# Causal mask added to the diagonal score blocks of four heads in one VectorE operation, row maxima taken two heads at a time from the masked scores

## What is computed

```
scale = D ** (-0.5)
scores = jnp.einsum('bqhd,bkhd->bhqk', sq, sk) * scale
causal = jnp.tril(jnp.ones((n, n), dtype=bool))
scores = jnp.where(causal[None, None], scores, jnp.finfo(scores.dtype).min)
attn = jax.nn.softmax(scores, axis=-1)
y = jnp.einsum('bhqk,bkhd->bqhd', attn, sv)
o = 0.5 * y + 0.5 * o_gla
```

## Time and profile before

| | |
|---|---|
| median of 3 runs | 945.17 us (944.21 to 946.2) |
| the profiled execution | 944.21 us, of which the trace spans 941.6 us |
| PE busy | 901.8 us (96%) |
| PEld busy | 712.3 us (76%) |
| DVE busy | 678.3 us (72%) |
| ACT busy | 661.8 us (70%) |
| POOL busy | 635.0 us (67%) |

### The profile page before, as it was taken

How to read it: one execution, slowest core, us unless ns; L and a number is a source line. 1 busy time by engine, 2 the same in 40 slices (tenths; PEclk the granted TensorE clock), 3 DMA queues, 4 the chain that set the end, 5 groups by cost and what they waited for, 6 DMA issues and landing times. The chain is left out here.

```text
span 941.6 us, 18334 instructions
## 1 busy us (share of the span) xinstructions
PE 901.8 (96%) x5145; PEld 712.3 (76%) x5145; DVE 678.3 (72%) x2016; ACT 661.8 (70%) x2146; POOL 635.0 (67%) x603
## 2 busy tenths in 40 slices
PE   7899999999999999999999999999999998888997
PEld 4677778787777777777777777787777766677886
DVE  4877867676767676768686969786888857574447
ACT  6687777777777777777776868687776766333655
POOL 6967676767666667677786767877676988443441
PEclk9999999999999999999999999999999999997999
DMA  7101100000000000710000001001003111133347
GB/s 263 35 12 29 29 24 1 6 13 8 1 0 0 0 0 7 210 28 1 1 2 1 1 1 43 1 2 32 1 17 105 62 39 57 57 109 95 109 126 232
DMA packets 30969, 41.46 MB, mean 44 GB/s; under 512 B 3230, under 2 KB 25631, under 8 KB 30624
## 3 DMA queue, kind: packets, MB, share of 16 engines
q1 hardware_dynamic: 27472, 31.98, 11.5%
q0 software_dynamic: 3408, 8.43, 2.5%
HBM read 24.72 MB, written 16.59 MB: 44 GB/s over the span
## 5 line engine op out<-in xcount | busy, mean ns | idle before, releaser
L1662 POOL TENSOR_TENSOR qd<-eqk,eg 128x512 f32<-128x512 f32 x63 | 75.0, 1190 | 133.2 <-issue 128.6
L631 PE MATMUL OA<-wT,V 128*128 128x512 f32 x320 | 149.2, 597 | 0.0
L847 ACT ACTIVATE S<-S,nm 128x128 f32<-128x128 f32 (+3 forms) x256 | 126.4, 494 | 8.2 <-DVE nm L1082 7.4
L1082 DVE CUSTOM_DVE_ANT_0 S<-S,maskb 128x128 f32<-128x128 f32 (+3 forms) x256 | 118.2, 518 | 15.2 <-PE S L585 12.3
L885 ACT ACTIVATE eqk<-qkv,nmx 128x128 f32<-128x128 f32 x320 | 124.3, 396 | 4.5 <-DVE nmx L1157 4.4
L1650 POOL TENSOR_TENSOR eqk<-eqk,rse 128x640 f32<-128x640 f32 x63 | 79.5, 1262 | 60.2 <-DVE rse L1200 37.0
L631 PEld LDWEIGHTS OA<-wT,V 128*128 128x128 f32 x320 | 59.7, 191 | 68.9 <-issue 68.9
L1116 DVE TENSOR_TENSOR pr<-S,rl 128x256 f32<-128x256 f32 (+3 forms) x128 | 105.5, 825 | 4.5
L1639 POOL TENSOR_TENSOR rp<-qkv,cos 128x640 f32<-128x640 f32 x64 | 99.5, 1555 | 7.7 <-ACT qkv L875 7.7
L1642 POOL TENSOR_TENSOR rp<-rp,rt 128x640 f32<-128x640 f32 x64 | 99.4, 1553 | 5.0
L1639 POOL TENSOR_TENSOR rt<-qkv,sin 128x640 f32<-128x640 f32 x64 | 99.3, 1552 | 0.0
(11 more groups left out here) (265 smaller groups left out, 2451.7 us busy)
## 6 DMA issues: line engine op xcount, KB each, us to landing
qkv<-slot_x SPq DMA_DIRECT2D x39, 129.0 KB
slot_x<-zero SPq DMA_DIRECT2D x3, 1290.0 KB, 15.3
stage<-in_wgu SPq DMA_DIRECT2D x8, 352.0 KB, 3.1
stage<-in_wqkv SPq DMA_DIRECT2D x6, 384.0 KB, 3.9
xraw<-in_x_cols SPq DMA_DIRECT2D x16, 128.0 KB, 2.5
acc<-in_x_rows SPq DMA_DIRECT2D x1, 2048.0 KB, 10.8
dn_w<-in_wdn SPq DMA_DIRECT2D x1, 2048.0 KB, 8.1
pr<-plane SPq DMA_DIRECT2D x8, 256.0 KB
```

Source lines behind the costliest of these rows:

```text
L631: last = pe.matmul(OA[:, :], V[:, j, :], wT[:, j, :], start=(c == 0 and j == 0), stop=(j == c))
L847: nc.scalar.activation(S[:, h, 0:n], S[:, h, 0:n], ACT.Exp, bias=nm[:, h:h + 1], scale=-1.0, accum_out=ls[:, h:h + 1]).then_inc(s_exp, 1)
L1082: nc.vector.tensor_tensor_reduce(out=S[:, h, 0:n], in0=S[:, h, 0:n], in1=maskb[:, N - n:N], scale=-1.0, scalar=FAR, op0=ALU.add, op1=ALU.m ...
L1662: nc.gpsimd.tensor_tensor(qd[:, par, 0:512].rearrange("p (h d) -> p h d", d=128), eqk[:, par, 0:512].rearrange("p (h d) -> p h d", d=128), ...
```

## The change

The four calls of `score_max` in a unit become one call of `mask_scores` and two of `score_max`. `mask_scores` adds the triangular block to the diagonal blocks of all four heads in one tensor operation (128 x 4 x 128 elements, in place in PSUM) and waits for the scores of all four heads. `score_max` is a plain row maximum over the n columns of two heads, with the sign turned, that waits for the mask. The custom operation with its accumulator read-out is gone, and ACT's exp no longer negates its input. In units c = 0, `o_low` of the group before, which stood between heads 1 and 2, now stands ahead of the mask.

```
-                    act.wait_ge(s_nm, 4 * u + 1 + h)
-                    nc.scalar.activation(S[:, h, 0:n], S[:, h, 0:n], ACT.Exp, bias=nm[:, h:h + 1], scale=-1.0,
+                    act.wait_ge(s_nm, 4 * u + 1 + h)
+                    nc.scalar.activation(S[:, h, 0:n], S[:, h, 0:n], ACT.Exp, bias=nm[:, h:h + 1],
                                          accum_out=ls[:, h:h + 1]).then_inc(s_exp, 1)
...
-            def score_max(g, c, h):
+            def mask_scores(g, c):
+
+                u = C * g + c
+                d = slice(P128 * c, P128 * (c + 1))
+                dve.wait_ge(s_sc, 4 * u + 4)
+                later(dve, s_exp, 4 * u)
+                nc.vector.tensor_tensor(S[:, :, d], S[:, :, d], maskb[:, N - P128:N].rearrange("p (o t) -> p o t", o=1)
+                                        .to_broadcast([P128, GQ, P128]), ALU.add).then_inc(s_mk, 1)
+
+            def score_max(g, c, pair):
 
                 u = C * g + c
                 n = P128 * (c + 1)
-                dve.wait_ge(s_sc, 4 * u + 1 + h)
-                later(dve, s_exp, 4 * u)
-                nc.vector.tensor_tensor_reduce(out=S[:, h, 0:n], in0=S[:, h, 0:n], in1=maskb[:, N - n:N], scale=-1.0,
-                                               scalar=FAR, op0=ALU.add, op1=ALU.min, accum_out=nm[:, h:h + 1]).then_inc(s_nm, 1)
+                h = slice(2 * pair, 2 * pair + 2)
+                dve.wait_ge(s_mk, u + 1)
+                nc.vector.tensor_reduce(nm[:, h], S[:, h, 0:n], AX_X, ALU.max, negate=True).then_inc(s_nm, 2)
...
                 if c:
                     update_state(g, c)
+                if c == 0 and not first:
+                    o_low(g - 1, C - 1)
+                mask_scores(g, c)
                 score_max(g, c, 0)
                 score_max(g, c, 1)
-                if c == 0 and not first:
-                    o_low(g - 1, C - 1)
-                score_max(g, c, 2)
-                score_max(g, c, 3)
```

More of the change, by code:

```diff
@@ L267, in layer_kernel @@
         s_sc, s_nm, s_exp, s_rl, s_pn = (sem(n) for n in ("s_sc", "s_nm", "s_exp", "s_rl", "s_pn"))
+        s_mk = sem("s_mk")
         s_at, s_am, s_pt, s_wta, s_wtd = (sem(n) for n in ("s_at", "s_am", "s_pt", "s_wta", "s_wtd"))
```

## The result

| | before | after |
|---|---|---|
| median | 945.68 us (944.21 to 947.31) | 1004.77 us (1002.7 to 1005.7) |
| span of the profiled execution | 941.6 us | 1002.3 us |
| mean granted TensorE clock | 0.988 | 0.976 |
| PE busy / DVE busy | 901.8 / 678.3 us | 922.2 / 717.9 us |

The ratio is 1.062, with a 95% interval of 1.061 to 1.064. The kernel is 59 us slower; 38 were forecast, and the time lies above the range. I cut both traces into the 64 units, at the first score matmul of each. The start of unit 63 moved by 60.5 us. The table gives what the units became longer, and what the prediction had for them (units 0 to 58, and the tail apart).

What follows compares the result with a forecast made beforehand. PE was taken as the bound. New waits 26.3 (c = 3) + 7.3 (c = 2) + 1.6 (c = 0) + 1.1 (c = 1) + 1.6 (tail) = 38 us gave 983 us; 8 in 10 is 971 to 1000.

Steps and rivals of the forecast that it cites:

- PE sets the pace, and each new wait adds its length: Mid-attention PE is busy 99.69 of 100 us, so every wait it lacks today adds its length to the time.
- Unit c = 3, 1.9 us: Mask waits for head 3, so `gc` comes late and PE waits 1.9 us ahead of L604; fourteen units, 26.6 us.
- the clock falls after the new stops: Rival, chance 0.26: TensorE's clock drops behind c = 3 stops, 1.5 us each; 994 us if half, 1004 if all.
- Unit c = 1, "nothing", hidden by 0.4 us: First exp waits for ACT's other work, hiding mask and maximum by 0.4 us; only two router-late units pay, 0.55 each.
- What is queued behind: Later work on DVE, ACT and POOL: `qd` stays ready, 0.1 to 0.2 us early in c = 0; DVE gets 0.4 us more per unit.
- Unit c = 0, 0.06 us: `gc` ends just after L604's present start: 0.06 us in fifteen units, 0.7 in unit 0, 1.6 in all.
- Any tenth more on DVE or ACT in c = 0 shows: Cover in c = 0 is gone after the change, so any further tenth there shows in the time.
- Unit c = 2, 0.65 us: Second `pr` ends later, so L613 waits 0.65 us in eight units and 0.3 on average in seven: 7.3 us.
- The tail, 1.6 us: From group 14's last unit POOL and a DMA also hold PE: of 4.9 us new waits, 1.6 remain.
- Smaller waits: Rival, chance 0.10: mask and maxima at lower bounds, c = 3 costs 1.6 and c = 2 0.4; 974, down to 965 us.
- a gain: Rival, chance 0.04: the wait is covered and PE's present waits on DVE go, or fewer operations save time; 940 to 945 us.
- no change: Rival, chance 0.04: exps are late for other reasons in all units, as in c = 1; 945 us.

Runs made afterwards that it cites:

- the filler: Changed kernel, in c = 3 the gated matrix moved behind the projection and five matmuls of zeros put into PE's stop: 996.07 us, ratio 1.053.
- the run with c = 1 alone: Kernel before with the new form (one mask, maxima of two heads) in units c = 1 only: 948.27 us, ratio 1.003.
- The control run: Changed kernel with the gated matrix of units c = 3 moved behind the projection, without added matmuls of zeros: 1003.86 us, ratio 1.063.
- the run with `gc` first: Changed kernel with the clamp of the gate sums ahead of both normalisations in every unit: 985.45 us, ratio 1.042.

## Why the prediction was wrong in size

*PE sets the pace, and each new wait adds its length.* Right. PE went from 99.69 to 94.36 busy us in 100, in stops released by `gc` and `pr`.

*Unit c = 3, 1.9 us.* The mechanism and the place were right, and the size nearly: 1.9 in the first two units, 2.1 in the others, 2.7 us more in 14 units. Three small terms were short. From the end of the mask to the maximum, two instructions of one engine with a semaphore between them, it is 0.10 us (322.63 to 322.73), where I put 0.03; from `gc` to L605 0.06; and the twelve matmuls of L605 take 1.52 us behind a stop, where they took 1.42.

*The rival "the clock falls after the new stops".* **This is the step that failed**, as I weighed it: "Against it: 1.78 is the nearer row." The sum of 983 us puts the clock at nothing, and it cost 11.5 us in c = 3; without these the time would lie inside the range. My stops came out at 1.84, and behind 7 of 15 the clock fell; 0.26 was too small a chance, and its 1.5 us a unit is 1.6 to 1.7. In the changed kernel and the two other runs with stops of 1.84 to 1.87 us in c = 3, 23 of 45 brought the clock down. In the five runs whose stops in c = 3 were at most 1.27 us, none of the 75 did. That it is the stop is shown by the filler: same waits, same arrival of `gc`, no fall.

The row of 1.78 us was read rightly, but it did not hold for c = 3. Its stop, in unit 2, is 1.51 to 1.82 us long in all fourteen traces, and the clock fell behind none of them. Nor does the length of a stop decide alone elsewhere. Behind the stop for `qd` in unit 60, 1.98 to 2.29 us in six traces, the clock fell in four; in unit 57 it fell in the runs with first stops of 1.50 and 1.58 us, each with a second of 0.79, and in two of the three with 1.84 and 0.80. Among equal stops, their place in time goes with what happens. In each trace all low stretches begin whole multiples of one interval apart. Of the 26 stops of 1.84 to 1.87 us in c = 3 that begin in about one half of that interval, 23 brought the clock down, and of the 19 in the other half none. I chose the halves after looking, and no run moves a stop on purpose, so this is a regularity of the traces and not a shown cause.

*Unit c = 1, "nothing", hidden by 0.4 us.* Right in its result by itself, as the run with c = 1 alone shows, and wrong in the kernel. Even there the cover is at most 0.1 us and not 0.4: I let the mask start where the first maximum did, at 1.55 us of the unit, but it waits for the fourth head until 1.70, and from mask to maximum it is 0.10 us and not 0.03. A second step failed here as well, in "What is queued behind": I followed the later gate exps of c = 0 to POOL's `qd` and asked if PE waits for it. It does not. But the rotation behind `qd` moved too, and it holds DVE's `gl` at the head of c = 1, so that the mask comes 0.7 us later still and the cover is overdrawn by up to 0.6. That is 3.0 us in groups 0 to 12. Another 3.8 are in units 53 and 57, sized at 0.55 each: in 57 DVE is so late that PE stops 1.84 us for `Ut` as well, and the clock falls. The control run has the same two stops there without a fall, and its unit 57 is 0.8 us shorter, so about 0.8 of the 3.8 is the clock.

*Unit c = 0, 0.06 us.* Too small: 0.20 typically, 0.52 in the units of groups 4 to 6. "Any tenth more on DVE or ACT in c = 0 shows" was the right warning. The handoff of 0.10 us instead of 0.03 is one such tenth, and the first matmuls behind the stop another. In groups 4 to 6 L605 begins 0.3 us after `gc` ends and not 0.05; why is open. That `gc` is what PE waits for there is shown by the run with `gc` first: 0.0.

*Unit c = 2, 0.65 us.* Measured 0.80, a stop of 0.58 released by `pr` and a slower start behind it.

*The tail, 1.6 us.* Right: units 59 to 62 are 1.4 us longer, though one of them has a fallen clock. PE's wait for `qd` in unit 60, 2.25 us, is gone, and with it the fall of the clock behind it; other waits took part of its place.

*Smaller waits, a gain, no change.* None happened. The Trainium skill, "VectorE: DVE Perf Modes", section "Rules for kernel authors", has the rule to minimise the number of operations. The runs show the other side here: eight rows of the trace became three, DVE's busy time rose by 39.6 us, and the form with two masks and two maxima (four rows), the first of which waits for two heads only, is 37 us faster than the one with three. Of the 39.6 us, 21 are in mask and maxima, 0.33 a unit where I had 0.4, and 9 are `gl` being held.

The 60.5 us by which the start of unit 63 moved are, in round figures: 31 of waiting in c = 3, about half of it the wait for head 3 and half the second pass and the pairs; 11.5 of clock in c = 3; 9 of c = 2; 5 of c = 0; 7 of c = 1, with 0.8 of clock; less 2.3 given back in units 60 to 62 and 0.3 by an earlier start. The medians lie 59 us apart. No version tried is faster than the kernel before.

## What to carry to other kernels

Joining per-head operations into one saves fixed costs on the engine that does them, and moves the start of everything behind to the arrival of the last input; where each head's chain ran beside the production of the next, that is the larger number, and it has to be read on the engine that sets the pace and not on the one that is relieved. Price a new stop of TensorE with the clock too: a harmless stop of about the same length at another place in the kernel proves little, even if it is harmless in every run, and a few matmuls in the stop tell at once how much of a loss is the clock. Where two delays each fit under their cover, ask whether they share it.

## What the hardware showed that I had not expected

- *A DVE operation held by a POOL operation.* `gl` reads two tiles of SBUF. With POOL's `rp` addition (two SBUF inputs, 1.56 us) running, it ended 0.14 to 0.15 us after POOL's did, however short its own 0.28 us, and took up to 1.19 us in the units c = 1 of groups 1 to 12; an operation of DVE that reads PSUM and SBUF, `oT_lo`, kept its 0.68 to 0.69 beside POOL operations with two SBUF inputs (37 times in the traces of before and after). The Trainium skill, "SBUF — State Buffer", section "Who interferes with whom", says that DVE's second SBUF port pair is shared with GpSimd and locked exclusively; the trace agrees. The hold had been there in before as well, with `gl` at 0.54 us in unit 26 and 1.30 in unit 61, and PE did not stop for it.
- *The clock after equal stops.* Of 45 stops of 1.84 to 1.87 us in units c = 3, 23 were followed by some microseconds partly or mostly at the lower level, about 1.6 us lost each time; in the 75 units c = 3 of the five runs with shorter stops (0.25 to 1.27 us) there was none. Outside c = 3 there are falls behind shorter stops, down to 1.50 us followed by 0.79 in unit 57, and stops of up to 2.19 us without one.
- *A semaphore between two instructions of one engine.* From end to start it was 0.10 us on DVE from mask to maximum, in all 64 units, and 0.03 us from the reciprocal to `pr`, in all 128 pairs. Where DVE did not wait, the next row began about 0.08 us before the end of the one ahead. The mask writes PSUM and the reciprocal SBUF; whether that makes the difference is not shown.
